# A depthwise convolution in a state space stage: from multiply-adds on VectorE to diagonal products on TensorE

## What is computed

```python
xz = h @ in_proj_w.T
x, z = jnp.split(xz, 2, axis=-1)
xpad = jnp.pad(x, ((0, 0), (D_CONV - 1, 0), (0, 0)))      # D_CONV = 4
xc = conv_b
for k in range(D_CONV):
    xc = xc + xpad[:, k:k + L, :] * conv_w[:, k]
xc = jax.nn.silu(xc)
x_dbl = xc @ x_proj_w.T                                   # dt, B, C
...
dt = jax.nn.softplus(dt @ dt_proj_w.T + dt_proj_b)
deltaA, deltaBu = exp(dt * A), dt * xc * B                # for 16 states n
h_t = deltaA * h_(t-1) + deltaBu                          # scan along the tokens
y = sum over n of h * C;  y = (y + D * xc) * silu(z);  out = y @ out_proj_w.T
```

## Time and profile before

| | before |
|---|---|
| median of 3 runs | 3355.52 us (3349.78 to 3358.53) |
| the profiled execution | 3378.07 us, its span 3376.3 us |
| VectorE busy | 2045.4 us, 61% of the span |
| TensorE busy | 2582.9 us, 76% |
| ScalarE busy | 1050.8 us, 31% |
| GpSimd busy | 1383.4 us, 41% |
| mean granted clock of TensorE | 0.871 |

### The profile page before, as it was taken

One profiled execution on the slowest core, in us unless ns is written; L12 is line 12 of the kernel. 1 busy time (PEld: TensorE's weight loads), 2 busy tenths in 40 slices (PEclk: granted clock), 3 DMA queues, 4 the chain that ended last, 5 costly groups with the idle time before them and its releaser, 6 DMA issues. The chain is left out here.

```text
span 3376.3 us, 35979 instructions
## 1 busy us (share of the span) xinstructions
PE 2582.9 (76%) x11915; PEld 1782.3 (53%) x11946; DVE 2045.4 (61%) x3652; ACT 1050.8 (31%) x1621; POOL 1383.4 (41%) x865
## 2 busy tenths in 40 slices
PE   6555299945799999996276767767677665997998
PEld 2222166644799999996122333323233233665997
DVE  8999867554112211213898898989999895332211
ACT  4544122200111111111445554455454531221111
POOL 0000034425333333332058677686777862112332
PEclk8777699965899999998588888888888887998999
DMA  3000100010799999886200100100100000115996
GB/s 107 0 0 0 42 7 19 12 33 26 278 325 326 323 326 326 321 307 224 80 26 25 38 25 26 38 25 26 38 26 25 38 25 19 38 38 183 348 350 241
DMA packets 90562, 395.00 MB, mean 117 GB/s; under 512 B 20854, under 2 KB 48006, under 8 KB 63840
## 3 DMA queue, kind: packets, MB, share of 16 engines
q1 hardware_dynamic: 68864, 351.46, 29.4%
q0 software_dynamic: 21600, 42.37, 3.5%
HBM read 364.94 MB, written 39.29 MB: 120 GB/s over the span
## 5 line engine op out<-in xcount | busy, mean ns | idle before, releaser
L1236 POOL TENSOR_TENSOR ss_h<-ss_h,ss_cs 128x2048 f32<-128x2048 f32 x128 | 578.8, 4523 | 89.3 <-DVE ss_h L1589 81.4
L1310 PE MATMUL ss_y<-ss_h,all_ident 128*128 128x512 f32 x1024 | 528.7, 665 | 21.0 <-POOL ss_h L1236 14.1
L1092 DVE TENSOR_TENSOR experts_in<-experts_sil,experts_pU 128x512 f32<-128x512 f32 x176 | 121.0, 687 | 652.5 <-PE experts_pU L1036 611.2
L1589 DVE TENSOR_TENSOR_SCAN ss_h<-ss_da,ss_c_h,ss_dbu 128x512 f32<-128x512 f32 x384 | 470.8, 1268 | 44.3 <-ACT ss_da L1440 38.4
L1310 PEld LDWEIGHTS ss_y<-ss_h,all_ident 128*128 128x128 f32 x1024 | 220.5, 218 | 294.9 <-issue 278.0
L1440 ACT ACTIVATE ss_da<-ss_dt,ss_decay 128x512 f32<-128x512 f32 x512 | 326.5, 710 | 144.9 <-DVE ss_h L1589 86.9
L1036 PE MATMUL experts_pG<-experts_xt,experts_wa 128*128 128x128 f32 x2816 | 346.6, 277 | 0.4 <-DMA experts_wa<-in_w_all 0.3
L1036 PE MATMUL experts_pU<-experts_xt,experts_wa 128*128 128x128 f32 x2816 | 343.9, 275 | 0.0
L1045 PE MATMUL experts_pY<-experts_wa,experts_in 128*128 128x256 f32 x1408 | 332.7, 379 | 0.0
L1036 PEld LDWEIGHTS experts_pG<-experts_xt,experts_wa 128*128 128x128 f32 x2816 | 331.4, 193 | 1.4 <-DMA experts_wa<-in_w_all 0.6
L1582 DVE TENSOR_TENSOR ss_dbu<-ss_dtx,ss_bB 128x1024 f32<-128x1024 f32 x256 | 314.5, 1228 | 28.6 <-PE ss_bB L1300 1.3
(11 more groups left out here) (321 smaller groups left out, 3717.9 us busy)
## 6 DMA issues: line engine op xcount, KB each, us to landing
experts_wa<-in_w_all SPq DMA_DIRECT2D x176, 1536.0 KB
ss_cs<-ss_c_rows SPq DMA_DIRECT2D x32, 1024.0 KB, 4.6
moe_rows<-route_xn SPq DMA_DIRECT2D x16, 512.0 KB
all_x<-in_x SPq DMA_DIRECT2D x8, 512.0 KB, 9.3
gf_xb<-in_x SPq DMA_DIRECT2D x8, 512.0 KB, 3.8
ss_h<-moe_ys SPq DMA_DIRECT2D x4, 1024.0 KB, 7.0
moe_rows<-all_x SPq DMA_DIRECT2D x8, 512.0 KB, 3.3
experts_xr<-moe_rows,moe_token POOLq DMA_INDIRECT x176
```

What stands on the lines that cost most here:

```text
L1092: nc.vector.tensor_tensor(IN[t.two][:].rearrange("p f t -> p (f t)"), SIL[t.two][:], pU[t.two][:], ALU.mult)\
L1236: pool.tensor_tensor(h[:], h[:], CS[q % 2][:, n % GROUP].unsqueeze(1).to_broadcast([P, CI, BT]), ALU.mult)\
L1310: mm = pe.matmul(y[:, c], ident[:], H[n % RING][:, c], start=(n == 0), stop=(n == N - 1))
L1589: ins = V.tensor_tensor_scan(H[n % RING][:, c], DA[n % 2][:, c], DBU[:, c % 2], first, ALU.mult, ALU.add)
```

## The change

The convolution becomes four matmuls for each group on TensorE: at the start ScalarE writes 16 diagonal matrices TAP[:, c, t] (the identity times conv_w of tap t, 128x128 each). convolve(b, c) multiplies the columns t to t + 511 of XR by TAP[:, c, t] and sums the four in the same PSUM bank. silu_x is called once for each group, reads PSUM, adds the bias and writes XC. It has two waits, conv_raw and then skip_done. VectorE's convolve and ScalarE's L1398 are gone. LN1 now lies in XR, and the second Routing object shares three small tiles with the first.

```diff
...
+            self.expert, self.token, self.place = before.expert, before.token, before.place
...
+        TAP = m_.sb("tap", [P, CI, TAPS, P])
...
-        ZS, LN1 = m_.sb("zs", [P, CI, BT]), m_.sb("ln1", [P, CI, BT])
+        ZS, LN1 = m_.sb("zs", [P, CI, BT]), XR[:, :, TAPS - 1:]
...
-                        wait(pe, "conv_done", b * CI + c)
+                        wait(pe, "xc_done", b * CI + c)
                     project(bank(b, c), WI, c * P, HT[b % 2], KD).then_inc(s["x_raw"], 1)
+
+                def convolve(b, c):
+                    wait(pe, "xr_done", b * CI + (c + 1))
+                    for t in range(TAPS):
+                        mm = pe.matmul(bank(b, c), TAP[:, c, t], XR[:, c, t:t + BT], start=(t == 0), stop=(t == TAPS - 1))
+                    mm.then_inc(s["conv_raw"], 1)
...
-                    wait(pe, "xc_done", b + 1)
+                    wait(pe, "xc_done", b * CI + CI)
...
-                            wait(pe, "conv_done", (b + 3) * CI)
+                            wait(pe, "xc_done", (b + 3) * CI)
...
-                wait(pe, "conv_done", CI)
+                wait(pe, "taps_done", 1)
+                for c in range(CI):
+                    convolve(0, c)
...
+                        if prep and n in (1, 2, 3, 4):
+                            convolve(b + 1, n - 1)
...
+                    for t in range(TAPS):
+                        tap = A_(TAP[:, c, t], ident[:], ACT.Copy, scale=conv_w[:, c, t:t + 1])
+                tap.then_inc(s["taps_done"], 1)
...
-                    q = bank(b, c)
-                    A_(XR[:, c, TAPS - 1:], q, ACT.Copy).then_inc(s["xr_done"], 1)
-                    wait(act, "xr_done", b * CI + (c + 1))
-                    A_(q, q, ACT.Identity, scale=conv_w[:, c, TAPS - 1:], bias=conv_b[:, c:c + 1]).then_inc(s["x_done"], 1)
-
-                def silu_x(b):
-                    wait(act, "conv_done", b * CI + CI)
-                    A_(XC[b % 2][:], XC[b % 2][:], ACT.Silu).then_inc(s["xc_done"], 1)
-                    A_(XR[:, :, 0:TAPS - 1], XR[:, :, BT:], ACT.Copy, scale=0.0 if starts_at(b + 1) else 1.0)
+                    A_(XR[:, c, TAPS - 1:], bank(b, c), ACT.Copy).then_inc(s["xr_done"], 1)
+
+                def silu_x(b, c):
+                    wait(act, "conv_raw", b * CI + (c + 1))
+                    wait(act, "skip_done", (b - 1) * CI)
+                    A_(XC[b % 2][:, c], bank(b, c), ACT.Silu, bias=conv_b[:, c:c + 1]).then_inc(s["xc_done"], 1)
+                    A_(XR[:, c, 0:TAPS - 1], XR[:, c, BT:], ACT.Copy, scale=0.0 if starts_at(b + 1) else 1.0)
...
-                        if prep and n == 6:
-                            silu_x(b + 1)
...
+                        if prep and n in (2, 3, 4, 5):
+                            silu_x(b + 1, n - 2)
...
-                pre.link(V.memset(XR[:], 0.0))
+                pre.link(V.memset(XR[:, :, 0:TAPS - 1], 0.0))
...
-                PER = CI * (TAPS - 2) + 2
-
-                def convolve(b, c):
-
-                    ch = Chain(dve, s["steps"], b * PER + c * (TAPS - 2))
-                    wait(dve, "x_done", b * CI + (c + 1))
-                    for t in range(TPB - 1):
-                        q = bank(b, c)
-                        out = q if t < TAPS - 2 else XC[b % 2][:, c]
-                        ins = V.scalar_tensor_tensor(out, XR[:, c, t:t + BT], conv_w[:, c, t:t + 1], q, ALU.mult, ALU.add)
-                        if t < TAPS - 2:
-                            ch.link(ins)
-                    ins.then_inc(s["conv_done"], 1)
...
-                    convolve(0, c)
-                    add_experts(c + 3)
-                add_experts(NB - 1)
+                for b in range(3, NB):
+                    add_experts(b)
...
-                        if prep and n in (2, 3, 4, 5):
-                            convolve(b + 1, n - 2)
...
```

More of the change, by code:

```diff
@@ L608, with __init__ @@
 class Routing:
-    def __init__(self, nc, stack, tag, experts, k, width, out=None):
+    def __init__(self, nc, stack, tag, experts, k, width, out=None, before=None):
         m_ = Memory(nc, stack, tag)
@@ L618, in __init__ @@
         self.weight = m_.sb("weight", [P, NT, k])
-        self.expert = m_.sb("expert", [1, P], I32)
-        self.token, self.place = m_.sb("token", [P, P], I32), m_.sb("place", [P, P], I32)
+        if before is None:
+            self.expert = m_.sb("expert", [1, P], I32)
+            self.token, self.place = m_.sb("token", [P, P], I32), m_.sb("place", [P, P], I32)
+        else:
+            self.expert, self.token, self.place = before.expert, before.token, before.place
         self.direct = out is not None
@@ L1134, in state_space @@
         s = {n: m_.sem(n) for n in (
-            "loaded", "sel_steps", "decay_done", "pre", "stats_ready", "steps", "h_done", "t_raw", "ht_done", "x_raw", "x_done",
-            "z_raw", "z_done", "conv_done", "xc_done", "zs_done", "xp_raw", "bc1_done", "bc_done", "dt_raw", "u_done", "exp_done",
+            "loaded", "sel_steps", "decay_done", "pre", "stats_ready", "steps", "h_done", "t_raw", "ht_done", "x_raw",
+            "z_raw", "z_done", "taps_done", "conv_raw", "xc_done", "zs_done", "xp_raw", "bc1_done", "bc_done", "dt_raw", "u_done", "exp_done",
             "ln_done", "tail", "dt_done", "dtx_done", "spread", "da_done", "dbu_done", "scanned", "pr_done", "summed", "c_stored",
@@ L1447, in _ @@
                     copy_x(0, c)
-                silu_x(0)
+                for c in range(CI):
+                    silu_x(0, c)
                 copy_bc(0)
@@ L1539, in first_steps @@
                         V.tensor_tensor(DTX[0][:, part], u, XC[0][:, part], ALU.mult).then_inc(s["dtx_done"], 1)
-                PER = CI * (TAPS - 2) + 2
-                def convolve(b, c):
-                    ch = Chain(dve, s["steps"], b * PER + c * (TAPS - 2))
-                    wait(dve, "x_done", b * CI + (c + 1))
-                    for t in range(TPB - 1):
-                        q = bank(b, c)
-                        out = q if t < TAPS - 2 else XC[b % 2][:, c]
-                        ins = V.scalar_tensor_tensor(out, XR[:, c, t:t + BT], conv_w[:, c, t:t + 1], q, ALU.mult, ALU.add)
-                        if t < TAPS - 2:
-                            ch.link(ins)
-                    ins.then_inc(s["conv_done"], 1)
+                PER = 2
                 def split_bc(b):
-                    ch = Chain(dve, s["steps"], b * PER + CI * (TAPS - 2))
+                    ch = Chain(dve, s["steps"], b * PER)
                     wait(dve, "bc1_done", b + 1)
@@ L1598, in _ @@
                 add_experts(2)
-                for c in range(CI):
-                    convolve(0, c)
-                    add_experts(c + 3)
-                add_experts(NB - 1)
+                for b in range(3, NB):
+                    add_experts(b)
                 split_bc(0)
@@ L1631, in build @@
         X = m_.sb("x", [P, NT, D])
-        r0, r1 = Routing(nc, stack, "moe0", 64, 2, D), Routing(nc, stack, "moe1", 16, 1, 2 * D, out)
+        r0 = Routing(nc, stack, "moe0", 64, 2, D)
+        r1 = Routing(nc, stack, "moe1", 16, 1, 2 * D, out, before=r0)
         with ExitStack() as inner:
```

## The result

| | before | after |
|---|---|---|
| median | 3356.15 us of 4 runs (3349.78 to 3358.53) | 3328.03 us of 4 runs (3326.78 to 3328.72) |
| the profiled execution | 3378.07 us, span 3376.3 | 3328.72 us, span 3326.9 |
| VectorE busy | 2045.4 us | 1977.0 us |
| TensorE busy | 2582.9 us | 2664.2 us |
| ScalarE busy | 1050.8 us | 1095.8 us |

The ratio is 0.9919, with a 95% interval of 0.9902 to 0.9936: 28 us faster, between 21.5 and 33. VectorE lost 68 us of work and TensorE gained 81, so less than half of what VectorE was relieved of came off the time.

A forecast was written before the change was run, and what follows sets the result against it. VectorE was taken to bound steps 2 to 5 of blocks 0 to 6. Of 8.2 us freed a block, 4.0 go to new waits: 29.6 us in seven blocks plus 3.2 before the loop, 33 us; median 3322 us, range 3298 to 3350.

The forecast's parts named there:

- The bound, and what is removed: Steps 2 to 5, blocks 0 to 6: VectorE sets the pace; removing its convolves frees 8.2 us a block, 57 us.
- The loop: TensorE and ScalarE, per group: x_part 1.71, add_up 3.43, convolve 3.60, silu 0.75, hand-overs about 0.1; 9.6 us.
- The load: ScalarE's silu table load, 1.28 us, waits only for skip_done and lies beside add_up and convolve for c = 1 to 3.
- rival (2): Table load in the loop, after both waits: loop 10.9 us, nothing gained in blocks 1 to 6, 3348 us; chance 11%.
- The stalls and the sum: Block 1: VectorE waits 1.5 and 1.9 us for the spread, 0.55 for out_part; steps 2 to 8 take 53.3 us.
- the 4.2 us a block: Steps 2 to 8: net gain per block, 8.2 us freed less 4.0 us of new waits; 29.6 us over seven blocks.
- Before the loop: Ahead of the loop: block 0's convolve moves to TensorE, x_proj runs faster, tap copies fit ScalarE's wait; 3.2 us gained.
- After step 8: Loop past step 8 of a block: both kernels issue the same work, TensorE has caught up, so the gain stays.
- The wait at split_bc: Past step 8: a possible new wait of split_bc for x_proj, with only some 0.7 us to spare, would show error.
- (1): Rival: VectorE stays the only bound, with a loop of 7.7 us; 60 us gained in all, 3295 us; chance 8%.
- (3): Rival: a table switch on ScalarE costs twice what the load shows, loop 11.1 us; 7 us slower, 3362 us; chance 5%.
- (4): Rival: TensorE's clock falls after silu waits, 1.6 us each; 3386 us on top of rival (2), 3360 otherwise; chance 8%.

The follow-up runs named there:

- experiment 5: Changed kernel with three of four convolution taps left out and one Silu over all groups at n = 6: 3319.4 us in a single execution, kernel before 3371.76.
- experiment 4: Changed kernel with one convolution tap in place of four, so the convolution isn't computed: 3317.09 us, ratio 0.9875 to the kernel before.
- experiment 7: Changed kernel with convolve(1 to 3) issued between the two halves of their step's add_up: 3327.54 us, ratio 0.9856 to the kernel before.
- Experiment 1: Changed kernel with silu_x's two waits swapped, skip_done first and conv_raw last: 3373.39 us, ratio 1.005 to the kernel before.
- experiment 8: Changed kernel with only block 0's convolution on TensorE, blocks 1 to 7 convolved on VectorE as before: 3373.52 us, ratio 0.9997 to the kernel before.
- experiment 9: The changed kernel unaltered, repeated on a third chip: 3346.01 us, ratio 0.9921 to the kernel before.
- experiment 2: Changed kernel with only the bias applied per group and one Silu over all four at n = 6: 3334.03 us, ratio 0.9934 to the kernel before.
- experiment 10: Changed kernel with convolve(1 to 3) inside add_up, rerun on the third chip beside the unaltered change: 3324.99 us, ratio 0.9857 to the kernel before.
- experiment 6: Changed kernel with convolve(c - 1) ahead of x_part(c), add_up cut in two around x_part, silu_x and copy_x moved: 3353.89 us, ratio 0.9989 to the kernel before.

## Why the prediction was right, step by step

**The bound, and what is removed.** Right. Step 2 fell to 10.09 us (10.1 said), steps 3 to 5 to 7.70 wherever TensorE is in time, and experiment 5 shows all of it at once: 57.5 - 49.3 = 8.2 us a block, when nothing else is late.

**The loop.** Right at 9.63 us for 9.6, by errors that cancel. Silu took 0.69 us, not the 0.75 of L1398, x_part 1.83 from start to start (1814.49 to 1816.32) for 1.71, and the two hand-overs 0.03 and 0.05 (silu starts at 1823.38, where the convolve ends at 1823.35, and x_part at 1824.12): 1.83 + 3.43 + 3.60 + 0.69 + 0.08 = 9.63. That this loop sets the pace, and not VectorE, is what experiments 4, 5 and 7 show, each with a loop shortened in another way: 8.55, 7.70 and 8.80 us.

**The load.** Right, and it carried the most: the reading of the earlier trace rows, by which the wait written last holds the load up. Experiment 1 reversed the order and put the load into the loop, 10.97 us for the 10.9 of rival (2). In experiment 4 a loop of 8.55 us holds two loads of 1.28 us, and what stands in front of and behind each is 0.01 to 0.03 us away. The Trainium skill, "ScalarE: Activation LUTs", section "What ACT_TABLE_LOAD costs", puts a switch at some 2.66 us; an estimate from this figure gives that loop 0.6 + 2.6 + 0.7 of work, 5.3 of switches and 2.0 of x_part, 11.2 us. The trace does not agree: a switch costs 1.3 us here.

**The stalls and the sum.** Said: 1.5, 1.9 and 0.55 us, 53.3 us for steps 2 to 8. Measured: 1.88, 2.06, 0.57 and 53.65. Seven blocks gave 27.5 us for 29.6. The step that was off is "block 0 has no add_skip and no out_part, its sum comes out alike". Block 0 gave 2.8, and so did block 4 (2.9), which the prediction did not set apart. VectorE's step is 7.46 us in these two, not 7.70, while the loop of TensorE and ScalarE stays at 9.63, so that each step adds more waiting. Timeline of VectorE of the kernel after, block 0:

```profile
1693.53 1.23 DVE L1587 TENSOR_TENSOR ss_dbu<-ss_dtx,ss_bB 128x1024 f32<-128x1024 f32 x1 [2.31 <-PE ss_bB L1310]
```

The three waits are 0.96, 2.31 and 2.30 us, 5.6 together, where block 1 waits 4.5. Blocks 2 and 5 gave more than was said, 5.1. In the kernel before, VectorE waited there for add_up in front of add_skip, as this row of its timeline, block 2, shows:

```profile
1982.52 2.72 DVE L1568 SCALAR_TENSOR_TENSOR ss_dtx<-ss_xc,ss_skip,ss_y 128x512 f32<-128x512 f32 x4 [1.07 <-PE ss_y L1310]
```

The x_part and the add_up in front of it were slow on a low clock (3.12 us against 1.88, 4.10 against 3.60). That wait is not in the kernel after, though nothing in the diff was meant for it. Nor is it in experiment 8, which keeps these steps on VectorE (57.5 and 57.6 us in blocks 2 and 5), and it is back in block 3 of experiment 7 (52.49 us against 51.32). So these 2.4 us (58.71 against 57.53, twice) look like scatter of the clock in the trace before, not like a gain of the change; without them the seven blocks gave 25.1 us, and the 27.5 stand nearer to the forecast by luck. Against the 4.2 us a block: -1.4 twice, +0.9 twice, and -0.3 in the other three, whose stalls were somewhat longer than said.

**Before the loop.** 3.7 us for 3.2. Timelines of the kernel after, ScalarE and then TensorE, in answer to the earlier trace rows:

```profile
1577.59 4.77 ACT L1395 ACTIVATE ss_tap<-all_ident,ss_conv_w 128x128 f32<-128x128 f32 x16
1583.35 2.08 ACT L1405 ACTIVATE ss_hn<-all_x,ss_shift,ss_rstd 128x256 f32<-128x256 f32 x4 [0.98 <-DVE ss_decay L1601]
```

```profile
1598.66 13.90 PE L1280 MATMUL ss_y<-ss_xr,ss_tap 128*128 128x512 f32 x32
1613.35 3.70 PE L1257 MATMUL ss_q<-ss_xc,ss_wx 128*128 128x512 f32 x8 [0.78 <-ACT ss_xc L1418]
```

The 16 tap copies took 0.30 us each, 4.77 together, and ScalarE still waited 0.98 us for VectorE behind them: hidden, with that much to spare. Block 0's convolves took 13.9 us for 13.7. x_proj took 3.70 us after a busy stretch, where it took 5.61 before.

**After step 8.** Both kernels were said to issue the same work there. The sum is right, 678.3 us before and 677.6 after, but the parts are not equal. Step 0 of blocks 1 to 7 takes 72.1 us in all before and 64.3 after; steps 10 and 11 of blocks 0 to 6 take 129.1 before and 137.2 after. The repeat of the change (experiment 9: 61.9 and 138.2) shows the same shift, experiment 8 (74.4 and 122.5) does not. What VectorE waits for there is ScalarE's decays, up to 3.6 us before and 4.2 after. The forecast had no term for either, and they cancel; why they moved was not looked into, so here too the sum is right by luck. The wait at split_bc, named as a danger, did not come.

**The rivals.** (1) fell: a loop of 7.7 us wants both the loads and three taps of four away (experiment 5). (2) was not what this kernel does; as a mechanism it was right (10.97 us), but its time of 3348 us was not, since it was priced apart from (4). Experiment 1 shows the two to be one: a wait 1.3 us longer brings falls of the clock with it, and the kernel comes out slower than before, 3373 us. (3) fell with experiments 2 and 4. (4) did not come: all 24 instructions of TensorE behind a wait for silu in blocks 1 to 6 of the kernel after ran at the high level, 1.98 us for an x_part, 3.69 for an out_part.

**The time.** 33 us of gain were said; the traces show 27.5 + 3.7 + 0.7 = 31.9 in this stage, the medians 28, with 21.5 to 33 as interval. 2 us of what is missing are the blocks' sum; the difference between 31.9 and 28 is within the measurement.

## What to carry to other kernels

Moving work from the bounding engine to another one pays only down to the longest loop that runs through the others: write that loop out as a sum (here 9.63 us against VectorE's 7.70), and then ask which of its members can stand beside another. Moving one call so that the silu lay under half an add_up gave 21 us more (experiments 9 and 10); moving more in the same spirit gave everything back, since work that had filled a gap was gone and out_part stood further back in its queue (experiment 6). And with an activation function that needs a table, the order of two wait lines decides whether its 1.3 us are free or in the loop. Here the waits of TensorE that they made were followed by a lower clock in 11 places (experiment 1), which cost as much again.

## What the runs showed of the hardware that was not expected

**More work, a faster clock.** With the convolve in the gaps, TensorE is more often at its high level: over block 1 the granted clock is 0.93 (again in experiment 9), before it was 0.87, and with one tap of four it is 0.89 and 0.87 (experiments 4 and 5). The place counts too: with all four taps in the order of experiment 6 it is 0.88. In block 0 the kernel before ran its first two x_parts on the low level, the second as this row of its timeline of TensorE shows; the kernel after ran its first in 3.39 us and the other three in 1.98.

```profile
1698.69 3.62 PE L1253 MATMUL ss_q<-ss_ht,ss_wi 128*128 128x512 f32 x4
```

So matmuls moved to a waiting TensorE cost less than their sum: 115 us of convolves were added (100.8 in the loop, 13.9 ahead of it), and its busy time rose by 81 us (the trace of the kernel before lacks some 30 more of its matmul records, so the rise is no larger than that). What decides over a single fall stays open: gaps of 0.45 to 0.65 us were followed by none in the kernel after and by four in experiment 1, gaps of 1.9 to 2.0 us there by seven of 18, and in experiment 4 the falls came behind the shortest gaps and behind the last ones.

**20 us elsewhere.** The profiled executions of the kernel before and of the kernel after differ by 49 us, the medians by 28. The other 20 lie before the change, in the routing of the first experts (700 to 900 us): VectorE's first instruction for the experts starts at 871.3 us in one, at 851.4 in the other. Waits in that window, before and then after:

```profile
PE route_pR L774 <- DVE route_oh L866: 37.2, 8, 10.5
...
DVE route_junk L885 <- remote: 21.3, 4, 5.4
```

```profile
PE route_pR L777 <- DVE route_oh L869: 17.1, 8, 3.7
```

TensorE waits 37.2 us instead of 17.1 for the same VectorE line, and in the slow case alone a releaser is named "remote". All profiled executions on the second and third chip show the late start (869 to 874 us), with whatever kernel, the change among them; those on the first (experiments 1, 2, 4 and 6) do not. So in these runs it goes with the chip, not with the kernel. On which chip the kernel before was profiled is not known; 20 us would be most of the 22.6 by which the profiled execution of the kernel before lay above its median. What it is stays open; no experiment was made on it.
